# A routed feed-forward / recurrent block on one core: router products widened to 128 columns, idle products in the early waits, and a new plan

## The reference

```
x = x + 0.5 * ffn(layernorm(x), router_w, expert_fc, expert_proj)
x = x + attn(layernorm(x), Wi, bi, Wh, bh)
x = x + 0.5 * ffn(layernorm(x), router_w, expert_fc, expert_proj)

attn: xi = x @ Wi.T + bi;  h_t = tanh(xi_t + h_(t-1) @ Wh.T + bh), t = 0..511
ffn:  e(token) = argmax(x @ router_w.T)          # one of 8 experts
      out(token) = square(relu(x @ fc[e])) @ proj[e]   # 128 -> 512 -> 128
```

## Time and profile before

| | |
|---|---|
| median of 3 runs | 580.89 us (580.31 to 581.51) |
| the profiled execution | 578.79 us |
| its span, first to last instruction | 576.4 us |
| mean granted clock of TensorE | 0.950 |
| busy: PE, PEld, DVE, ACT, POOL | 532.8, 520.4, 405.9, 315.4, 450.0 us |
| instructions | 15923 |

### The profile page before, as it was taken

One profiled execution on the slowest core, in us unless ns is written; L12 is line 12 of the kernel. 1 busy time (PEld: TensorE's weight loads), 2 busy tenths in 40 slices (PEclk: granted clock), 3 DMA queues, 4 the chain that ended last, 5 costly groups with the idle time before them and its releaser, 6 DMA issues.

```text
span 576.4 us, 15923 instructions
## 1 busy us (share of the span) xinstructions
PE 532.8 (92%) x4541; PEld 520.4 (90%) x4541; DVE 405.9 (70%) x1485; ACT 315.4 (55%) x1104; POOL 450.0 (78%) x562
## 2 busy tenths in 40 slices
PE   6849998899999999999999999999999999988991
PEld 6848997899999999999999999999999999877991
DVE  4799486778686798697569865777586467784650
ACT  2222363556666666566665666666656665544560
POOL 2497887559898887088997989978998938899982
PEclk8666599999999999999999999999999999999996
DMA  7974822222222232133323333322332301435410
GB/s 246 274 267 167 253 89 69 74 67 74 75 68 86 73 79 62 39 93 108 93 65 79 106 110 100 91 61 75 93 103 80 108 20 70 144 125 143 115 40 0
DMA packets 54147, 58.88 MB, mean 102 GB/s; under 512 B 8983, under 2 KB 42018, under 8 KB 54064
## 3 DMA queue, kind: packets, MB, share of 16 engines
q1 hardware_dynamic: 43776, 36.15, 21.4%
q0 software_dynamic: 9440, 21.06, 11.6%
q10 hardware_dynamic: 848, 0.66, 0.5%
HBM read 27.67 MB, written 30.62 MB: 101 GB/s over the span
## 4 chain that ended last, share of the span: by engine, by line
PE 71%; POOL 8%; DVE 8%; issue 5%; DMA 3%; SPq 1%; ACT 1%; POOLq 0%; ACTq 0%; DVEq 0%
PE yp L1705 23%; PE hp L1695 22%; PE z L1715 11%; PE mT L1601 4%; PE xTp L1684 4%; POOL idle L1166 3%; POOL xy_dram L1183 3%; PE lg L1645 3%; PE z L1665 2%; POOL out_dram L1203 2%; DMA hsT<-in_L_attn_x_dram 2%; ACT s_sb L1513 1%; PE hp L1720 1%; DVE pay L1252 1%; DVE r_sb L1375 1%
## 5 line engine op out<-in xcount | busy, mean ns | idle before, releaser
L1705 PE MATMUL yp<-projT,s_sb 128*128 x1248 | 204.0, 292 | 8.5 <-ACT s_sb L1513 8.2
L1695 PE MATMUL hp<-xT_sb,w_sb 128*128 128x128 f32 x1248 | 200.7, 289 | 0.3 <-ACT w_sb L1504 0.2
L1705 PEld LDWEIGHTS yp<-projT,s_sb 128*128 128x128 f32 x1248 | 164.1, 193 | 10.9 <-issue 10.8
L1695 PEld LDWEIGHTS hp<-xT_sb,w_sb 128*128 128x128 f32 x1248 | 166.0, 196 | 1.7 <-issue 0.5
L1484 ACT ACTIVATE hsT<-z 128x16 f32<-128x16 f32 x512 | 93.7, 183 | 134.1 <-PE z L1715 124.4
L1715 PE MATMUL z<-hsT,wT 128*128 128x16 f32 x1024 | 156.7, 229 | 0.1
L1715 PEld LDWEIGHTS z<-hsT,wT 128*128 128x128 f32 x1024 | 153.7, 190 | 3.2 <-ACT hsT L1484 0.3
L1513 ACT ACTIVATE s_sb<-r_sb 128x256 f32<-128x256 f32 (+1 forms) x260 | 114.2, 452 | 63.0 <-DVE r_sb L1375 31.6
L1375 DVE TENSOR_SCALAR r_sb<-hp 128x512 f32<-128x512 f32 x156 | 106.9, 685 | 56.9 <-PE hp L1695 54.8
L1166 POOL MEMSET idle<- 128x600 f32 x229 | 141.8, 619 | 0.2
L1504 ACT ACTIVATE w_sb<-fc_sb 128x256 f32 (+1 forms) x259 | 112.8, 455 | 4.6 <-issue 2.2
(11 more groups left out here) (133 smaller groups left out, 502.4 us busy)
## 6 DMA issues: line engine op xcount, KB each, us to landing
xs_sb<-xs_dram SPq DMA_DIRECT2D x71, 129.0 KB, 2.2
xy_dram<-zeros SPq DMA_DIRECT2D x11, 512.0 KB, 5.1
xs_sb<-xy_dram SPq DMA_DIRECT2D x85, 64.0 KB, 1.9
xy_dram<-y_sb SPq DMA_DIRECT2D x85, 64.0 KB, 1.6
hsT<-in_L_attn_x_dram SPq DMA_DIRECT2D x14, 256.0 KB
hsT<-n_L_ffn_expert_proj_dram SPq DMA_DIRECT2D x2, 1024.0 KB, 16.3
fc_sb<-in_L_ffn_expert_fc_dram SPq DMA_DIRECT2D x1, 2048.0 KB
out_dram<-y_sb,xs_sb POOLq DMA_INDIRECT x71, 2.6
```

The source lines that it names most:

```text
L1695: mm = pe.matmul(hp[:, g % 2, h * P:(h + 1) * P], w_sb[:, g % 2, h * P:(h + 1) * P], xT_sb[:, g % 2, :], start=True, stop=True)
L1705: mm = pe.matmul(yp[:, 0:D], s_sb[:, g % 2, h, :], projT[:, bass.ds(offsets[g] + h * D, D)], start=(h == 0), stop=(h == HC - 1))
```

## The change

- The router weights get 120 zero columns behind their 8 (`wT` is P columns wider, zeroed by one more POOL memset), and each logits product moves 128 columns instead of 8 (fewer only where the bank of 512 would end). The zeros land in columns of `lg` that later products overwrite or nobody reads. The planner's model of these passes is told the same.
- `fill()` now counts the wait from the end of the last real or idle product (`worked`) and goes on until two tiles are ordered.
- The planner's model of the clock is another: the level follows the columns moved alone.
- While the last route has been picked and isn't scattered yet, a put is only taken if POOL would start it before a set time (`keep`).
- The DVE pieces of the last route may go ahead of the relu (`end`).
- `STEP`, `MIDDLE`, `AHEAD` and all weights in `PR` have new values, so beats and queues come out in a new order. SP now loads the second expert weights ahead of the rows of units 4 to 6 (units 4 and 5 came first before), and the first expert weights ahead of unit 7 (units 6 and 7 came first before).

```diff
-STEP = [1, 3, 1]
-MIDDLE = [1, 1, 1, 1, 1, 1, 1, 1, 1, 2, 2, 2, 1]
+STEP = [1, 2, 1]
+MIDDLE = [1, 1, 1, 1, 1, 1, 1, 1, 1, 2, 1, 2, 1, 1]
...
-PR = {'proj': -24.384, 'lat1': 38.464, 'lat2': 16.638, 'lat3': -13.853, 'last': 29.433,
-      'hor': 107.488, 'beat': 7.703, 'put': -24.921, 'dve': 2.201, 'act': 2.708, 'pe': 2.163,
-      'early': 0.283, 'load': 3.662, 'hold': -24.24, 'slack': 112.715, 'near': 0.036,
-      'tol': 0.127, 'mix': -7.274, 'late': 0.379, 'root': 80.609, 'gather': -101.48,
-      'scatter1': -8.609, 'scatter2': 11.874, 'crit': 18.133, 'front': 5.404, 'dvx': 1.683,
-      'burst': 0.3}
+PR = {'proj': -35.632, 'lat1': 26.48, 'lat2': 34.843, 'lat3': -33.661, 'last': -206.797,
+      'hor': 112.882, 'beat': 9.258, 'put': -24.742, 'dve': 2.201, 'act': 2.838, 'pe': 2.228,
+      'early': 0.409, 'load': 2.739, 'hold': -33.121, 'slack': 227.622, 'near': 0.101,
+      'tol': 0.104, 'mix': -9.084, 'late': 2.531, 'root': 53.268, 'gather': -109.337,
+      'scatter1': -72.076, 'scatter2': 7.508, 'crit': 18.159, 'front': 6.33, 'dvx': 1.1,
+      'burst': 0.3, 'keep': -2.212, 'end': 2.652}
-AHEAD = [2, 4, 7]
+AHEAD = [0, 3, 7]
...
-    SUB, SIG, WIDE, SLOW = 0.1115, 0.327, 0.09, 1.9
+    SUB, SIG, WIDE, SLOW, ACTIVE = 0.1115, 0.327, 0.09, 1.9, 12.2
...
             if start >= limit:
                 return
-            p = min((p for p in pool_wait if p[0] <= start), key=pool_urgency)
+            if ("pick", second[-1]) in ev and second[-1] not in sorted_out:
+                soon = [p for p in pool_wait if p[1][0] != "put" or max(pool_free, p[0]) < ev["pick", second[-1]] + PR["keep"]]
+                start = max(pool_free, min([p[0] for p in soon], default=limit))
+                if start >= limit:
+                    return
+            else:
+                soon = pool_wait
+            p = min((p for p in soon if p[0] <= start), key=pool_urgency)
...
-                clock = 0.5 if moved < 12 and clock == 1.0 else 1.0 if busy > 0.95 * WINDOW else clock
-                begun, busy, moved = begun + WINDOW, 0.0, 0.0
+                clock = 0.5 if moved < ACTIVE else 1.0
+                begun, moved = begun + WINDOW, 0.0
...
-                n = int((need[0] - pe) / 0.25) if not order else 0
+                nonlocal pe
+                n = int((max(need[0], pe) - worked) / 0.25) if len(order) <= 1 else 0
                 if n > 0:
                     b.idle[place] = n
+                    pe = worked
                     matmuls(2 * n, 128, 0.0)
...
-                    return passes(place, 4, 8, (("turn", p[1], p[2]), lg_after[p[1].index]), p if half else None)
+                    return passes(place, 4, 128, (("turn", p[1], p[2]), lg_after[p[1].index]), p if half else None)
...
-                hurry = isinstance(job[0], Middle) and (job[0].u0 * UNIT - t) * 0.66 < PR["crit"]
+                hurry = (job[0].u0 * UNIT - t) * 0.66 < PR["crit"] if isinstance(job[0], Middle) else job[0] and job[0].second and job[0].last and PR["end"] > 0
...
-        wT = sb("wT", [P, 2 * P + E])
+        wT = sb("wT", [P, 3 * P])
...
+            pool.memset(wT[:, 2 * P + E:], 0.0).then_inc(s_const, 1)
...
                 for q in (2 * half, 2 * half + 1):
-                    j = 4 * i + q
-                    mm = pe.matmul(lg[:, j * E:(j + 1) * E], xrt[:, m % XRING, q * P:(q + 1) * P], rwT, start=True, stop=True)
+                    at = (4 * i + q) * E
+                    n = min(P, 512 - at)
+                    mm = pe.matmul(lg[:, at:at + n], xrt[:, m % XRING, q * P:(q + 1) * P], wT[:, 2 * P:2 * P + n], start=True, stop=True)
```

More of the change, by code:

```diff
@@ L214, in plan @@
     turns_of, logits_of, est, held = [], [], {}, []
-    clock, begun, busy, moved = 1.0, 0.0, 0.0, 0.0
+    clock, begun, moved, worked = 1.0, 0.0, 0.0, 5.0
     def ahead_of(r):
@@ L367, in matmuls @@
     def matmuls(n, columns, need):
-        nonlocal pe, clock, begun, busy, moved
+        nonlocal pe, clock, begun, moved, worked
         at = max(pe, need)
@@ L372, in matmuls @@
             while at >= begun + WINDOW:
-                clock = 0.5 if moved < 12 and clock == 1.0 else 1.0 if busy > 0.95 * WINDOW else clock
-                begun, busy, moved = begun + WINDOW, 0.0, 0.0
+                clock = 0.5 if moved < ACTIVE else 1.0
+                begun, moved = begun + WINDOW, 0.0
             d = max(SUB, columns * 2 / 2400) * (1 if clock == 1.0 else SLOW)
-            busy, moved = busy + d, moved + columns / 128
+            moved += columns / 128
             end, at = at, at + d
-        pe = at
+        pe = worked = at
         return end + (SIG if clock == 1.0 else 0.5) + WIDE * min(1, columns / 128) * (1 if clock == 1.0 else SLOW)
@@ L1129, in _ @@
             pool.iota(kio_i[:, :], pattern=[[1, TILES2 + 1]], base=0, channel_multiplier=0).then_inc(s_const, 1)
-            pool.wait_ge(s_const, 8)
+            pool.wait_ge(s_const, 9)
             pool.affine_select(out=ident[:, :], in_=ident[:, :], compare_op=ALU.not_equal, fill=1.0, base=0,
@@ L1404, in add_states @@
                 dve.tensor_tensor(v, v, mT[:, :].rearrange("p (j d) -> p j d", d=D), ALU.add).then_inc(s_evac, 1)
-            dve.wait_ge(s_const, 17)
+            dve.wait_ge(s_const, 18)
             link(dve.tensor_copy(kio[:, :], kio_i[:, :]))
@@ L1731, in split @@
                     inputs(piece[1], half)
-            pe.wait_ge(s_const, 10)
+            pe.wait_ge(s_const, 11)
             warm_up(EARLY)
```

## The result

The changed kernel takes 578.28 us in the median of 20 runs (574.35 to 580.36), the kernel before 581.09 us (576.16 to 583.49, 20 runs) on the same chip. The ratio is 0.9955, 95% interval 0.9935 to 0.9975: 2.8 us or 0.45% faster. The forecast was 569.5 us, so about 8.8 us of the expected gain did not arrive. The experiments ran in four groups, each on one chip together with the kernel before, whose median lay between 576.65 and 577.63 us there. So kernels are compared by ratios to it, and directly only within a group.

A forecast was written before the change was run, and what follows sets the result against it. TensorE, busy 92% of the span, was taken as bound by its number of passes, with early windows at half clock. Terms +0.3 - 7.7 - 3.0 + 0.5 - 1.5 = -11.4 gave 569.5 us on the median's footing; range 560 to 578 us.

The forecast's parts named there:

- The clock of the first tiles, -7.7 us: First tiles' window, 56.1 to 72.4 us: wide logits and idle passes give full clock, 8.6 us instead of 16.3.
- Rival (c): Columns don't count: the clock stays at 0.5 in the first tiles' window, 577.2 us; chance 0.07.
- R0's decision, -3.0 us: While R0 is decided: earlier logits and place bring first scatter to 21.1 and move the first tile 3.0 us; bounds 0, -4.
- Wider logits, +0.3 us: Logits passes: 120 more columns cost nothing in pace at full clock, only some latency per group, +0.3 us.
- idle products, +0.5 us: Idle passes in PE's waits: overshoot may delay the product behind them, +0.5 us; bounds 0 and some 2 us.
- The first step, -10.7 us: Recurrence's start: tiles 3.0 + 7.7 us earlier let the first gather and first step move by 10.7; bounds 6.4, some 15.
- rival (b): POOL sets the recurrence's start: R2's power stays ahead of the gathers, start moves 6.4 us, 573.8 us; chance 0.12.
- The recurrence, 0 with 3 us either way: Long stretch: orders all new, PE's idle there 4.5 us in all, so 0, bounds -3 and +3.
- a recurrence longer than before: Sign of a wrong forecast: the early gain is given back in the new order.
- The rule that an earlier start comes out as an earlier end one for one: Long stretch, 116.7 to 489.6 us: PE is bound by number of passes, so an earlier start gives an equally earlier end.
- The tail, -1.5 us: Last route's decision: `keep` and place and list ahead of relu release the last tiles earlier, -1.5 us; bounds -5.0, +2.
- the far bound (+2): Tail: DVE's decision ahead of relu holds up a tile's square and second product, POOL idles while puts queue, +2 us.

The follow-up runs named there:

- two norms early: Kernel with the third route's head cut in two, plus R0's second and R1's first norm moved forward on DVE: 572.92 us, ratio 0.9909.
- The two other padded kernels in the old order: Kernel before with padded logits plus idle products in the waits: 575.46 us, ratio 0.9977; or plus the third route's head cut in two: 573.79 us, ratio 0.9943.
- the head cut: Changed kernel with the third route's head on DVE cut into two pieces, the second one tile later: 571.74 us, ratio 0.9913.
- the old tail: Last units' place and list behind relu, as in the kernel before; put back in the changed kernel alone: 573.02 us, ratio 0.9930.

## Why the prediction was wrong

**The clock of the first tiles, -7.7 us: right.** The window is at 1.00, and eight logits passes of 128 columns take as long as eight products of a tile (1.06 us). In the changed kernel's timeline two tiles' first products are 1.90 us apart, as I said they would be (the view ends within the second row):

```profile
63.71 1.06 PE L1707 MATMUL hp<-xT_sb,w_sb 128*128 128x128 f32 x8
...
65.61 0.63 PE L1707 MATMUL hp<-xT_sb,w_sb 128*128 128x128 f32 x4
```

The fourth tile begins its products at 63.71; it began at 72.48 before, 8.8 us later. Not every execution does as well: in three of the ten later profiles of this order with padding the window of the first tiles is at 0.90. Rival (c), that columns don't count, gives the time nearest to the one measured (577.2 us), and its mechanism is refuted by the kernel without padding. A time that fits says little about the cause.

**R0's decision, -3.0 us: the scatter moved, the tile did not.** The first scatter starts at 20.05 (21.1 forecast, rows 6). The chain from there was wrong. POOL's timeline of the changed kernel:

```profile
20.05 1.23 POOL L1193 DMA_INDIRECT xy_dram<-pay,pos  x1 [3.60 <-DVE pos L1308]
...
32.14 0.96 POOL L1193 DMA_INDIRECT xy_dram<-pay,pos  x1 [5.59 <-DVE pay L1262]
...
51.44 0.96 POOL L1193 DMA_INDIRECT xy_dram<-pay,pos  x1 [0.17 <-issue]
```

I had said that nothing in the change alters the pace of the sixteen scatters. A scatter also needs its rows normalised, and the new order moved R0's second norm on DVE behind the head and four list entries, to 30.75 us. The fifth scatter waits 5.59 us for it, and the last one is at 51.44, against 50.74 before. The norms that I took out of the decision's way came back as the next wait, and I had not looked for who needs them. Even with that mended (two norms early), with the last scatter at 45.92, the first tile starts not clearly earlier than in other profiles of this order (55.85 and 56.83 us, against 55.96 to 57.66).

**Wider logits, +0.3 us, and idle products, +0.5 us: nothing to be seen.** Neither cost can be told from 0, and the idle products' worth can't either: with padding alone the window of the first tiles is at 1.00 already.

**The first step, -10.7 us: it came 3.0 us earlier. This is the step that failed.** I carried the tiles' lead to the first gather and from there to the first step, 21.4 us behind it before. The first half held in the main: the first gather starts at 87.93 instead of 95.30, 7.4 us earlier, about what the clock was to give (7.7), with nothing from R0. POOL's order is neither the forecast's (gathers ahead of R1's last scatters) nor rival (b)'s (R2's power ahead of the gathers): R1's last scatter is at 85.48, and R2's power comes behind unit 0's gathers. The second half failed: from the first gather to the first step it takes 25.8 us. Three views of the changed kernel, POOL's, DVE's and PE's:

```profile
87.93 1.00 POOL L1207 DMA_INDIRECT back<-xy_dram,pos  x1 [0.88 <-DMA xy_dram<-y_sb]
...
94.59 5.47 POOL L1166 TENSOR_TENSOR rstd<-veps,half 128x32 f32<-128x32 f32 x1
...
101.00 1.04 POOL L1166 TENSOR_TENSOR rstd<-veps,half 128x4 f32<-128x4 f32 x1
```

```profile
104.55 1.60 DVE L1262 TENSOR_SCALAR pay<-pay,mv,rstd 128x128 f32<-128x128 f32 x4
```

```profile
107.59 0.71 PE L1717 MATMUL yp<-projT,s_sb 128*128 x4 [1.52 <-ACT s_sb L1523]
108.14 0.60 PE L1611 MATMUL mT<-ident,pay 128*128 128x128 f32 x4
```

Unit 0's power starts 13.1 us behind the first gather, much as before (12.8). From there to the turn of its rows it takes 7.1 us instead of 4.0, and from the turn to the first step 5.6 instead of 4.7. Unit 0's norm runs on DVE behind a norm of R2 (103.42 us) and ahead of the next relu, PE waits 1.52 us for squares behind that relu, and the turn comes after four products that need them. The kernel with the padding alone shows that the first gather doesn't carry the first step: its first gather is 4.3 us later than the changed kernel's, and its first step, at 111.6, 2.1 us earlier. The two other padded kernels in the old order have their gathers at 92.0 and 91.6 us and their first steps at 113.1 and 112.7, again no later than the new order's 112.2 to 114.4.

```profile
92.22 1.12 POOL L1198 DMA_INDIRECT back<-xy_dram,pos  x1 [0.19 <-issue]
```

PE's timeline of the changed kernel has no wait for unit 0 in it: its rows are turned at 108.14 and its products run from 110.02, each behind other work of PE. What fills the time up to the first step is PE's own passes and PE's waits for others. The passes from 56 us on are as many as before (431, 427): R2's last logits are now done ahead of the first tile, and tile passes have taken their place ahead of the first step. They take 6.3 us less, which is the clock, a little under the 7.7. The waits take 3.3 us more. PE's longer waits of the changed kernel from 56.0 to 113.7 us (total, times, longest):

```profile
PE yp L1717 <- ACT s_sb L1523: 4.7, 4, 1.5
PE xTp L1696 <- DMA xs_sb<-xy_dram: 2.5, 3, 1.5
PE xTp L1696 <- issue: 0.5, 2, 0.3
```

and those of before from 56.0 to 116.69 us:

```profile
PE yp L1705 <- ACT s_sb L1513: 4.2, 3, 1.7
PE xTp L1684 <- DMA xs_sb<-xy_dram: 0.9, 1, 0.9
```

The waits for squares, behind pieces of R2 on DVE, did not shrink with a faster clock, and PE waits longer for its first tiles' rows (the 0.9 us of before lie mostly ahead of 56.0). With the two norms early the waits for rows are gone from both profiles, and yet the first step, at 111.6 and 113.3 us, is not clearly earlier than the 112.2 to 114.4 without. So the chain through POOL, on which I had built the 10.7, did not set the first step. That PE's fixed order, with its passes and its waits for DVE, sets it in its place is read from the timelines; no run took its waits for squares away. What R0's 3.0 us would have brought, had they arrived, no run shows.

**The recurrence, 0 with 3 us either way: two terms of opposite sign.** Up to the first step PE now has 690 passes that are not idle products (864 less 174), and before it had 656 (688 less 32). These are missing between first and last step, where the profiles count 32 fewer: 3289 passes instead of 3321. With the head cut it takes 375.8 us, 3.2 less than before. With the head whole DVE holds PE for 1.68 us at 156 us, after which the clock may fall: 381.3 us in the first profile, 376.5 and 376.1 in the second and third profile of the same kernel, where it didn't. I had listed a recurrence longer than before as a sign that the early gain is given back, and the first profile does show it; the other two don't.

The rule that an earlier start comes out as an earlier end one for one does not hold well either. In the old order with padding the first step is 5.1 us earlier and the last one 2.8, with the same passes; with the two norms early the first step is 1.9 us earlier than with the head cut alone and the last one 0.7 later. The passes take 0.1132 instead of 0.1128 us in the former, spread over the whole stretch. I found no single place for it. As profiles of one order differ by 2 us, it may be no more than that; this stays open.

**The tail, -1.5 us: +1.4.** The last list is written 7 us earlier by the clock of the trace (511.91, rows 8), the four scatters end at 516.3, and the first tile with the last list is turned at 519.91 (before: 523.03). But DVE's timeline has place and list in one piece ahead of the next relu, and PE's has the consequence:

```profile
506.88 0.18 DVE L1285 TENSOR_TENSOR posw<-lg,total 128x32 f32<-128x32 f32 x1
...
511.91 0.18 DVE L1373 TENSOR_SCALAR list_i<-list_f 128x18 int32<-128x18 f32 x1
511.99 0.69 DVE L1385 TENSOR_SCALAR r_sb<-hp 128x512 f32<-128x512 f32 x1
```

```profile
513.53 2.07 PE L1717 MATMUL yp<-projT,s_sb 128*128 x8 [3.71 <-ACT s_sb L1523]
...
515.60 1.91 PE L1707 MATMUL hp<-xT_sb,w_sb 128*128 128x128 f32 x8
```

PE stands for 3.71 us and then runs at half clock. From the last step to the end the kernels with the new tail take 81.2 to 82.1 us in eight profiles, those with the old tail 79.9 to 80.7 in eight, before among them. In each of the first eight PE waits 3.3 to 3.7 us for these squares and its clock falls around it (0.57 to 0.79 in windows of 6 or 8 us); in each of the other eight the longest wait there is under 2 us and the clock stays at 1.00. I had this mechanism as the far bound (+2) of the term and took the other side.

**The sum again.** With the head cut: first step -3.2, recurrence -3.2, tail +0.7, so -5.7 us in the profiles and 0.9913 in the ratio (-5.0 us). Against the forecast's -11.4, three things are missing at the first step: R0's 3.0, 2.9 in longer waits, and 1.6 of the clock's gain (6.1 instead of 7.7). That is 7.5 us, or 6.7 after the 0.8 of costs that I had allowed for. In the tail 2.2 are missing. The 3.2 in the recurrence, which I had put at 0, came on top. The forecast came out too low because I let every gain at the front run through to the end and priced the new order at nothing. The changed kernel itself is 1.8 us slower than that in median, since in some executions the clock falls after the head's wait. Of its 20 runs the fastest (574.35 us) has a mean clock of 0.991, the slowest (580.36 us) 0.977.

## What to carry to other kernels

On an engine that is busy throughout, count its passes between the marks (first tile, first step, last step, end) and the idle time between them, before and after: what comes early on another engine gains nothing where the bound one has other passes in front. When work is moved out of the way of a decision, ask who needs the moved work next, and how long a piece it makes where it lands: DVE's piece of 4.05 us stopped PE for 1.68 us here, and one of 5.1 us for 3.71, while the head cut in two stopped it for no time that shows. And where a wait can cost the clock, its price is not its length: with 1.7 us of waiting the recurrence took less than 1 us longer where the clock stayed up, and 2.4 to 5.2 us longer than that where it fell.

## What the runs showed of the hardware

The granted clock did not follow how busy TensorE was. In the new order without padding it was 0.50 with PE busy 7.60 of 7.60 us (48.5 to 56.1 us), 27 of its 39 passes there being logits passes of 8 columns; with 128 columns in those passes it was 1.00 in the same window.

It also fell to 0.50 inside the recurrence of the changed kernel, where PE had been back to back for 39 us, after one wait of 1.68 us. It stayed there for about 6 us while PE was busy without a gap, two 16-column passes to four tile passes. Behind that wait (1.64 to 1.73 us) it fell in three of six profiles; what decides that, no run here tells. With the wait filled by 24 passes of 128 columns, or cut away, it did not fall there in any of six. With the waits of 3.3 to 3.7 us in the new tail it fell in eight of eight.
